# A vision-transformer tower on one core: images loaded one slot further ahead, and setup work of the start moved

## The reference

```python
patches = img.reshape(Bn, C, N_P, P, N_P, P)                 # 14 x 14 patches of 3 x 14 x 14
tokens = jnp.einsum('bsd,hd->bsh', patches, W) + b
h = jnp.concatenate([cls, tokens], axis=1) + pos             # 197 x 128 per image
# linear attention, written as a scan over the tokens
mem = jnp.einsum('bd,bde->be', q_t, state)
new_state = DECAY * state + LR * jnp.einsum('bd,be->bde', k_t, v_t)
h = h + outputs @ Wo + bo                                    # input: layernorm(h)
# routed attention: one of three weight sets per image, 8 heads, 8, 4 or 1 key/value heads
logits = jax.nn.relu(x.mean(axis=1) @ r_w1 + r_b1) @ r_w2 + r_b2
sel = jnp.argmax(jax.nn.softmax(logits, axis=-1), axis=-1)
out = gqa(x, *params[sel], nkv)                              # x = layernorm(h); softmax(q k / 4) v, then wo
h = h + out
```

## Time and profile before

| | |
|---|---|
| median of three timed runs | 989.46 us (986.82 to 997.56) |
| profiled execution | 983.08 us |
| its span, first to last instruction | 981.0 us |
| mean granted TensorE clock in it | 0.933 |
| busy: PE, PEld, DVE, ACT, POOL | 88%, 78%, 62%, 55%, 33% |
| share of the chain that ended last: PE, SyncE's queue, DMA, issue | 37%, 23%, 19%, 8% |
| ScalarE idle before L873 until the shift copies have landed | 118.9 us, 48 times |
| SyncE's queue: packets, share of 16 DMA engines | 124432, 61.4% |

### The profile page before, as it was taken

One profiled execution on the slowest core, in us unless ns is written; L12 is line 12 of the kernel. 1 busy time (PEld: TensorE's weight loads), 2 busy tenths in 40 slices (PEclk: granted clock), 3 DMA queues, 4 the chain that ended last, 5 costly groups with the idle time before them and its releaser, 6 DMA issues.

```text
span 981.0 us, 27005 instructions
## 1 busy us (share of the span) xinstructions
PE 866.9 (88%) x8112; PEld 764.2 (78%) x8112; DVE 611.6 (62%) x1956; ACT 539.5 (55%) x1300; POOL 321.2 (33%) x848
## 2 busy tenths in 40 slices
PE   1477779999999989799899998999989999999997
PEld 1466678888888878689789787879878888888785
DVE  2135566757676676467666667567756676677673
ACT  0234345566466655456556655556566466556565
POOL 1565433323333332223332434233333333332100
PEclk9979899979899999789998999799989898999899
DMA  6555677666766765665766676676667666754550
GB/s 170 154 152 151 142 180 174 167 155 167 166 166 162 170 172 150 160 157 151 167 169 161 153 178 167 152 166 171 166 153 171 168 160 152 184 120 85 107 119 19
DMA packets 128241, 150.98 MB, mean 154 GB/s; under 512 B 11838, under 2 KB 122574, under 8 KB 122702
## 3 DMA queue, kind: packets, MB, share of 16 engines
q1 hardware_dynamic: 124432, 147.86, 61.4%
q10 hardware_dynamic: 3646, 1.19, 0.7%
HBM read 30.99 MB, written 6.46 MB: 38 GB/s over the span
## 4 chain that ended last, share of the span: by engine, by line
PE 37%; SPq 23%; DMA 19%; issue 8%; DVE 4%; POOL 4%; ACTq 2%; ACT 1%; POOLq 1%; DVEq 0%
SPq L232 11%; DMA img<-in_x 10%; PE ps L420 6%; DMA img<-img 6%; PE ps L536 5%; PE ps L577 5%; SPq L253 5%; PE ps L560 5%; SPq L222 3%; DMA stack<-qk 2%; SPq L239 2%; PE ps L609 2%; PE ps L466 2%; SPq L244 2%; PE ps L509 2%
## 5 line engine op out<-in xcount | busy, mean ns | idle before, releaser
L786 DVE TENSOR_REDUCE top<-ps 99x2 f32<-99x394 f32 x512 | 268.7, 560 | 153.2 <-PE ps L536 151.1
L918 ACT ACTIVATE prob<-ps 99x396 f32<-99x396 f32 x512 | 229.2, 499 | 48.9 <-PE ps L560 47.1
L536 PE MATMUL ps<-stack 66*99 66x198 f32 x1024 | 207.2, 287 | 14.1 <-DMA stack<-qk 9.0
L560 PE MATMUL ps<-stack 68*99 68x198 f32 x1024 | 188.6, 268 | 33.6 <-ACT prob L918 33.2
L873 ACT ACTIVATE cols<-img 126x588 f32<-126x588 f32 (+1 forms) x128 | 135.0, 1057 | 128.7 <-DMA img<-img 118.9
L420 PE MATMUL ps<-w_tok,cols 126*99 126x128 f32 x1280 | 175.4, 290 | 12.4 <-ACT cols L873 12.4
L536 PEld LDWEIGHTS ps<-stack 66*99 66x99 f32 x1024 | 140.1, 174 | 57.9 <-issue 41.1
L560 PEld LDWEIGHTS ps<-stack 68*99 68x99 f32 x1024 | 138.5, 173 | 41.5 <-ACT prob L918 39.7
L420 PEld LDWEIGHTS ps<-w_tok,cols 126*99 126x99 f32 x1280 | 160.1, 181 | 12.6 <-issue 12.6
L577 PE MATMUL ps<-prob,v_ones 99*32 99x198 f32 (+1 forms) x2048 | 114.9, 342 | 0.4 <-ACT prob L918 0.4
L345 POOL TENSOR_TENSOR var<-mv,eps 99x2 f32<-99x2 f32 x64 | 12.7, 198 | 241.7 <-DVE mv L729 241.6
(11 more groups left out here) (142 smaller groups left out, 1475.9 us busy)
## 6 DMA issues: line engine op xcount, KB each, us to landing
stack<-qk SPq DMA_DIRECT2D x256, 198.0 KB, 5.2
img<-in_x SPq DMA_DIRECT2D x192, 150.1 KB
img<-img SPq DMA_DIRECT2D x64, 449.4 KB
img<-img SPq DMA_DIRECT2D x64, 448.5 KB
out<-h SPq DMA_DIRECT2D x64, 49.5 KB
out<-h SPq DMA_DIRECT2D x64, 49.0 KB
stack<-top_rows SPq DMA_DIRECT2D x64, 12.4 KB
w_rows<-in_L_tok_W SPq DMA_DIRECT2D x1, 294.0 KB, 3.1
```

The source lines that it names most:

```text
L536: last = nc.tensor.matmul(ps[0:T, M0 + c % 2, j * SP:(j + 1) * SP], stack[b.ring % 4][0:BIAS_ROW, h, 0, qt * T:(qt + 1) * T], stack[b.ring ...
L560: last = nc.tensor.matmul(ps[0:T, E0 + c % 2, j * SP:(j + 1) * SP], stack[b.ring % 4][:, h, 1, kt * T:(kt + 1) * T], stack[b.ring % 4][:, ...
L786: nc.vector.tensor_reduce(top[:, c // 4, 2 * (c % 4):2 * (c % 4) + 2], columns, AX.X, ALU.max, negate=True).then_inc(m_read, 1)
L918: nc.scalar.activation(prob[:, c, :], ps[0:T, E0 + c % 2, 0:CHUNK], ACT.Exp, scale=DK ** -0.5).then_inc(exp_done, 1)
```

## The change

Images are loaded two slots ahead of the shift in place of one: SHIFTED is 2 and every lag behind it grows by one, so that between the other steps nothing moves except in SyncE's list, where the load of an image now stands one slot earlier against everything else. Only the shift of image 0 is still made one slot after its load. 32 slots are written out ahead of the loop in place of 16 (PEEL). The weights of the second stage are loaded from SyncE's queue, four DMAs in each of four slots of the start; the scaling of `r_w1`, which waits for them, is done with image 4; the weight sets are built two slots ahead of the first routing; and the stack rows are set before GpSimd's first slot. Routing stays with the same images, so its conditions are written by image in place of slot.

```diff
+PEEL = 32
...
-    for n in range(RING):
+    for n in range(PEEL):
         slot(Image(n // RING, n % RING))
-    with engine.Fori(1, B // RING) as turn:
+    with engine.Fori(PEEL // RING, B // RING) as turn:
...
-SHIFTED, PATCHED, TURNED, ADDED, ROUTED = 1, 2, 3, 4, 8
-PROJECTED, STACKED, MAXED, TOPPED, MIXING, ENDING, STORED = 9, 10, 11, 12, 13, 14, 15
+SHIFTED, PATCHED, TURNED, ADDED, ROUTED = 2, 3, 4, 5, 9
+PROJECTED, STACKED, MAXED, TOPPED, MIXING, ENDING, STORED = 10, 11, 12, 13, 14, 15, 16
...
+            def ffn_weights(i):
+                set_of = sets[:, i * 4 * D:(i + 1) * 4 * D].rearrange("p (w e) -> p w e", w=4)
+                sp.dma_start(raw[i][0][:, :], ins[f"L0_ffn_wq{i}"]).then_inc(ffn_in, 16)
+                sp.dma_start(raw[i][1][:, :], ins[f"L0_ffn_wk{i}"]).then_inc(ffn_in, 16)
+                v_to = set_of[:, 2, :] if KV[i] == HEADS else raw[i][2][:, :]
+                sp.dma_start(v_to, ins[f"L0_ffn_wv{i}"]).then_inc(ffn_in, 16)
+                sp.dma_start(set_of[:, 3, :], ins[f"L0_ffn_wo{i}"]).then_inc(ffn_in, 16)
+
+            def routing_weights():
+                for to, name in ((r_w1, "r_w1"), (r_w2, "r_w2")):
+                    sp.dma_start(to[:, :], ins[f"L0_ffn_{name}"]).then_inc(ffn_in, 16)
+                sp.dma_start(r_b1[:, :], column(ins["L0_ffn_r_b1"])).then_inc(ffn_in, 16)
+                sp.dma_start(r_b2[:, :], ins["L0_ffn_r_b2"].rearrange("(a k) -> a k", a=1)).then_inc(ffn_in, 16)
+
             def slot(n):
-                plan = [(shift, n.back(SHIFTED)), (stack_up, n.back(STACKED)), (store, n.back(STORED)),
+                shifted = n.back(SHIFTED)
+                if isinstance(n.round, int) and n.i == 1:
+                    shifted = n.back(1)
+                if isinstance(n.round, int) and n.i == SHIFTED:
+                    shifted = Image(-1, 0)
+                plan = [(shift, shifted), (stack_up, n.back(STACKED)), (store, n.back(STORED)),
                         (bias_rows, n.back(TOPPED)), (load, n)]
                 for step, b in plan:
                     if b.exists():
                         step(b)
+                if isinstance(n.round, int) and 3 <= n.i < 3 + len(KV):
+                    ffn_weights(n.i - 3)
+                if isinstance(n.round, int) and n.i == 3 + len(KV):
+                    routing_weights()
...
             def set_stack_rows():
 
-                pool.wait_ge(kept, 1)
+                pool.wait_ge(pool_step, 9)
...
-                if isinstance(n.round, int) and n.i == PATCHED:
-                    set_stack_rows()
-                if isinstance(n.round, int) and n.i == TURNED:
+                if isinstance(n.round, int) and n.i == ROUTED - 2:
                     build_sets()
+            set_stack_rows()
             run_slots(pool, slot, TOPPED)
...
-                if not b.has(1):
+                if isinstance(b.round, int) and b.i == 4:
                     dve.wait_ge(ffn_in, 16 * 16)
...
-                routing = n.back(ROUTED) if n.ring % BATCH == 0 else Image(-1, 0)
+                routing = n.back(ROUTED) if n.back(ROUTED).ring % BATCH == 0 else Image(-1, 0)
...
-            for to, name in ((r_w1, "r_w1"), (r_w2, "r_w2")):
-                act.dma_start(to[:, :], ins[f"L0_ffn_{name}"]).then_inc(ffn_in, 16)
...
-            for i in range(len(KV)):
...
-                act.dma_start(set_of[:, 3, :], ins[f"L0_ffn_wo{i}"]).then_inc(ffn_in, 16)
```

More of the change, by code:

```diff
@@ L567, in mix_values @@
                     routed = b.back(ROUTED - MIXING)
-                    if b.ring % BATCH == (RING - MIXING) % BATCH and routed.exists():
+                    if routed.ring % BATCH == 0 and routed.exists():
                         pe.wait_ge(log_ready, batch_of(routed))
@@ L820, in slot @@
                 projected, maxed, ending = n.back(PROJECTED), n.back(MAXED), n.back(ENDING)
-                routing = n.back(ROUTED) if n.ring % BATCH == 0 else Image(-1, 0)
-                choosing = n.back(ROUTED + 1) if n.ring % BATCH == 1 else Image(-1, 0)
+                routing = n.back(ROUTED) if n.back(ROUTED).ring % BATCH == 0 else Image(-1, 0)
+                choosing = n.back(ROUTED + 1) if n.back(ROUTED + 1).ring % BATCH == 0 else Image(-1, 0)
                 plan = [(choose, choosing), (maximum, maxed, 0), (maximum, maxed, 1), (add_attention, added),
@@ L850, in _ @@
             nc.scalar.activation(w_vo[:, :], ps[:, CZ, D:2 * D], ACT.Copy).then_inc(w_vo_ready, 1)
-            for to, name in ((r_w1, "r_w1"), (r_w2, "r_w2")):
-                act.dma_start(to[:, :], ins[f"L0_ffn_{name}"]).then_inc(ffn_in, 16)
-            act.dma_start(r_b1[:, :], column(ins["L0_ffn_r_b1"])).then_inc(ffn_in, 16)
-            act.dma_start(r_b2[:, :], ins["L0_ffn_r_b2"].rearrange("(a k) -> a k", a=1)).then_inc(ffn_in, 16)
-            for i in range(len(KV)):
-                set_of = sets[:, i * 4 * D:(i + 1) * 4 * D].rearrange("p (w e) -> p w e", w=4)
-                act.dma_start(raw[i][0][:, :], ins[f"L0_ffn_wq{i}"]).then_inc(ffn_in, 16)
-                act.dma_start(raw[i][1][:, :], ins[f"L0_ffn_wk{i}"]).then_inc(ffn_in, 16)
-                v_to = set_of[:, 2, :] if KV[i] == HEADS else raw[i][2][:, :]
-                act.dma_start(v_to, ins[f"L0_ffn_wv{i}"]).then_inc(ffn_in, 16)
-                act.dma_start(set_of[:, 3, :], ins[f"L0_ffn_wo{i}"]).then_inc(ffn_in, 16)
             act.wait_ge(x_pads_ready, 1)
```

## The result

| | before | changed |
|---|---|---|
| median, 6 runs each | 989.24 us (986.82 to 997.56) | 881.82 us (879.07 to 889.05) |
| profiled execution, its span | 983.08, 981.0 us | 879.76, 877.9 us |
| mean granted clock | 0.933 | 0.974 |
| steady part, image 0's to image 49's output sum | 699.7 us, 14.28 a slot | 613.9 us, 12.53 a slot |
| image 0's output sum | 159.8 us | 141.7 us |

The ratio is 0.891, 95% interval 0.887 to 0.896: faster, by 107 us where 87 were forecast. Medians hold all executions; the ratios leave out single slow ones.

The account below looks back on a forecast made before the run. SyncE's full DMA queue, waiting for images to land, was taken as the bound. 983.1 us less 64 in the steady part and 24 in the fill, plus 6.4 from profiled execution to median, gave 902 us, range 882 to 937.

Parts of the forecast that it names:

- What bounds the kernel, and that the wait goes.: Steady part: SyncE's full queue sets the pace; its 2.91 us wait for the load goes, leaving 11.55 us a slot.
- TensorE's own pace is (2 x 11.8 + 13.6 + 13.6) / 4 = 12.7 us.: Steady part: TensorE is the next bound, averaging two plain slots, the routing slot and the one after: 12.7 us.
- I add 0.2 us a slot for stalls that stay.: Steady part: allowance for late shifts and the clock dips they bring, 10 us in all.
- The loop, 4 us.: Steady part: the one jump back left costs a 2.0 us wait plus about as much of low clock, 4 us.
- Weight loads off ScalarE's queue, 9.8 us.: Start: sixteen loads no longer precede the first columns, which start at 16.2 us; 9.8 us won, SyncE's issues cost 0.
- Stack rows, 6.1 us.: Fill: memsets moved to the start no longer hold back the normalisation of image 1; 6.1 us won.
- They now delay another slot by as much: 0, with 3 us either way.: Fill: 4.4 us of GpSimd's weight-set copies, built three images later, only shift their delay; 0, with 3 us either way.
- the 8 us for the end of the fill: End of the fill: shifts and stack copies come earlier, half the waits taken as won, 8 us, bounds 0 and 13.
- the low end: Whole run: lower end of the range, with fill 32 and no stall beyond 12.7 us a slot; 884, rounded 882.
- B, the load ahead of the shift: SyncE's queue: shift copies move only after the load drains, so 2.91 us return as latency; 927 us, chance 0.23.
- C, issues that grow: SyncE's queue: freed wait returns as longer issues, steady part stays at 14.3 us a slot; 965 us, chance 0.10.
- D, slower: Head of a slot: TensorE waits for stack copies queued behind load and shift, then low clock; 1030 us, chance 0.05.

Follow-up runs that it names:

- extra6: The changed kernel with six small DMAs more at the end of SyncE's list in each of slots 16 to 63; 911.45 us, ratio 0.931.
- extra3: The changed kernel with three small DMAs more at the end of SyncE's list in each of slots 16 to 63; 886.05 us, ratio 0.902.
- weights_back: The changed kernel with the sixteen weight loads issued by ScalarE ahead of its first slot again; 890.01 us, ratio 0.906.
- lag_only: The kernel before with the images loaded one slot further ahead and nothing else; 892.94 us, ratio 0.911.
- peel48: The changed kernel with 48 slots written out and a loop of one turn, never jumped back to; 876.02 us, ratio 0.890.

## Why the prediction came out as it did

- **What bounds the kernel, and that the wait goes.** Right, and shown: the wait alone put back brings the 14.2 us slots back. What SyncE needs, 11.55 us, was right too (11.5 by extra6).
- **"TensorE's own pace is (2 x 11.8 + 13.6 + 13.6) / 4 = 12.7 us."** This step failed, by the largest amount. The pace is 12.40: 11.84 twice, 13.12 and 12.78, so 49 x 0.30 = 15 us. The plain slots were read rightly. The two windows of 13.60 us in the earlier trace rows were taken for slots in which TensorE "had caught up", but in the last one it had been busy for 12.43 us only, so over 1 us of it was a wait. In the other it was busy for 13.34 us, more than the whole slot takes now; why its busy time was longer there is not shown.
- **"I add 0.2 us a slot for stalls that stay."** This term failed too, by its whole 10 us. The shift came in time, by 2.05 us at the median where the prediction had 1 to 2; the columns waited for it 1.2 us in 49 slots, and the granted clock of the steady part is 0.99. With 0.95 us more on the queue (extra3) the steady part hardly grew either.
- **The loop, 4 us.** 6.9 us in this trace, 7 us between kernels on one chip. The wait was put at 2.0 us, the longest of the earlier trace rows, and the low clock behind it at as much; now the one stop is 4.0 us and the clock adds 2.6. What was missed is that every engine, SyncE too, stops. Steady part: 15 + 10 - 3 = 22 us, which is the whole overestimate (636 for 613.9).
- **Weight loads off ScalarE's queue, 9.8 us.** 8.9 at the first columns (17.05 for 16.2 us). Of the other 0.9 us, 0.4 were gone in the trace with the memsets moved off VectorE's copies, which is within what traces of one start differ by. That the issues on SyncE cost nothing is not shown: the lead over weights_back is 9.7 us at the tokens of image 0 (23.50 for 33.21) and 7.8 at those of image 2. At most 2 us went there.
- **Stack rows, 6.1 us.** Right: 6.5 when undone.
- **"They now delay another slot by as much: 0, with 3 us either way."** This step failed, in the fill. In the kernel before the weight sets lay in the same gap as the memsets, which held the images back anyway; alone in a slot of 6.7 us that was running at full clock, they cost 3.9 us there and 1.2 to 3.3 behind it, by two traces of the same code. This is outside the 3 us either way. With it the fill is 18.1 in place of 24 us. What became of the 8 us for the end of the fill is not told apart: TensorE's waits for the stack copies there fell from 6.7 to 3.5 us, ScalarE's for the shifts stayed at 9.0.
- **Luck at the low end.** Its sum gives 884 us (32 of fill, 12.7 us a slot) and was set at 882. Against that sum the steady part came out 12 us shorter and the fill 14 us longer, and the median lay 2.1 us above the profiled execution in place of 6.4. That the measured 881.82 lies so close to the range is thus two errors that nearly cancel.
- **B, the load ahead of the shift.** Refuted. The shift lands 7.03 us after its issue at the median where it took 6.94, so of the 2.9 us that B wanted back 0.1 came. The Trainium skill ("DMA: Bandwidth & Descriptors", section on queues, rings and completion order) has the count of a DMA land only behind all earlier writes of the same DMA engine. The traces agree with this: in the changed kernel and in lag_only every shift of the steady part landed 2.4 us or more behind the load ahead of it. But 927 us do not follow from it, since the load lands 3.0 us after the shift's issue, and the shift took 6.9 also without one. Where the load itself was late the shift was late too, but those are six slots of 49. The prediction's sign for B, columns 9 to 10 us behind the issue, shows up in lag_only, in the few slots in which ScalarE waits at all. The time at hand was longer than forecast besides: from the first stack issue to the end of the load it took 9.0 us of the earlier trace rows, and here 7.8 (317.00 to 324.80), since the stack issues are shorter after a pause. 1.0 + 7.8 + 7.0 = 15.8 us, and the columns are wanted at 17.9 in plain slots.
- **C, issues that grow.** Refuted as a result: they became shorter (stack issues 2.6 us at the median for 3.9). Half of its reason may hold, though: in extra6, where SyncE doesn't pause, they are longer by 1.3 us. Whether the pause itself or the traffic in it makes the difference is not shown.
- **D, slower.** Refuted, no wait of TensorE for the stack copies.

## What to carry to other kernels

A load and its first use in one in-order issuing queue want a slot of other work between them. The wait takes its own length out of the queue in every round (2.8 us here), and it costs what the round then exceeds the next engine's pace by (14.2 less 12.5 us); put the wait alone back to see whether it is that. Read a latency from all its landings, not from the slots in which somebody waited for it: those are the late ones. Setup work that is moved is free only if it lands in a gap: ask what the new slot would do at full speed, and cut long pieces up. When such a bound falls, read the next engine's pace only from windows in which it is busy throughout, and then look at the loop's jump back, which no engine hides any more.

## What the runs showed of the hardware

- GpSimd's memsets slow VectorE's copies that run beside them: 14 copies of 128x42 take 3.95 us in place of 1.55, and one of 99x198 1.59 in place of 0.26, which is about the length of one memset (1.41 to 1.62). This fits the Trainium skill, "SBUF — State Buffer", section on the two separate sides of SBUF, by which the two engines share a pair of ports that one of them holds for a whole instruction.
- A copy (two DMAs, 42x2739 and 42x2734) issued 0.04 us behind a load of the same queue lands 7.0 us after its issue, as it does when that load has landed (6.9), although the load lands only 3.0 us after the copy's issue. Where the load lands 4.2 us or more after it (6 of 49), the copy takes 8.9.
- The same four stack DMAs take 2.6 us to issue after a pause of the queue and 3.9 us behind a load and a shift that were just issued. A DMA to one partition takes 0.31 us, one of the load's three 0.9 in the slots that are written out and 1.0 in the loop.
- A jump back of the loop stops all engines for some 4 us and is followed by 5.6 us of TensorE at 0.53 of its clock; entering the loop costs nothing (peel48).
- The fill of the same code ends between 138.2 and 147.3 us in eight traces: the slot behind the weight sets that ran at 0.68 of the clock in one trace had the full clock in another (10.73 and 8.63 us).
